# Adjacency tiles of 128 rows for the graph diffusion, and another table of how many diffusions stand in each block

## The reference

```python
R = S + jnp.eye(N); R = R / R.sum(-1, keepdims=True)
Z = 0; Xf = X; Xa = X
for n in range(2):
    probs = softmax((Xa @ W1.T @ W2.T) @ (Xa @ W3.T).T)
    A = probs * (in the top-p set of its row, p = 0.9);  A = A / A.sum(-1)
    Xf = R @ Xf                     # the diffusion, twice
    Xa = A @ Xa                     # the attention, twice
    Z = Z + Xf @ U1[n].T + Xa @ U2[n].T
```

## Time and profile before

| | |
|---|---|
| Time, median of 3 runs | 7123.94 us (7119.68 to 7130.17) |
| Profiled execution | 7131.35 us, its span 7129.6 us |
| Busy, share of the span | PE 64%, DVE 75%, ACT 30%, POOL 5% |
| Second attention pass | 1933 to 4957 us |
| TensorE clock granted, mean | 0.828 of full speed |
| L687, the diffusion's products | 834.5 us busy, 308.9 us idle before them, 301.1 of it until a DMA |

### The profile page before, as it was taken

One profiled execution on the slowest core, in us unless ns is written; L12 is line 12 of the kernel. 1 busy time (PEld: TensorE's weight loads), 2 busy tenths in 40 slices (PEclk: granted clock), 3 DMA queues, 4 the chain that ended last, 5 costly groups with the idle time before them and its releaser, 6 DMA issues. The chain is left out here.

```text
span 7129.6 us, 80171 instructions
## 1 busy us (share of the span) xinstructions
PE 4537.1 (64%) x27812; PEld 3255.7 (46%) x27812; DVE 5314.4 (75%) x13021; ACT 2161.8 (30%) x3033; POOL 344.0 (5%) x170
## 2 busy tenths in 40 slices
PE   5995688888665364523475588553337888835981
PEld 2442467676554354522464477453311222205981
DVE  4885577777448888887888899886349999974864
ACT  2332565656311011100132244222132222213541
POOL 0000000000110000000000000010000222020000
PEclk9997788888897787866787799786669999977995
DMA  5551000000032122111111122110103333303840
GB/s 171 202 199 57 1 2 1 1 1 1 21 132 97 57 86 85 75 40 43 58 66 57 50 87 93 59 58 17 29 16 130 107 110 109 110 26 144 292 161 29
DMA packets 192671, 549.28 MB, mean 77 GB/s; under 512 B 20027, under 2 KB 77126, under 8 KB 192126
## 3 DMA queue, kind: packets, MB, share of 16 engines
q1 hardware_dynamic: 187069, 539.58, 21.2%
q0 software_dynamic: 5120, 3.97, 0.2%
HBM read 526.73 MB, written 16.68 MB: 76 GB/s over the span
## 5 line engine op out<-in xcount | busy, mean ns | idle before, releaser
L655 PE MATMUL ps<-ident,arena 125*125 125x125 f32 x3200 | 562.9, 311 | 1161.4 <-DVEq L1139 1161.4
L655 PEld LDWEIGHTS ps<-ident,arena 125*125 125x125 f32 x3200 | 492.9, 224 | 1201.7 <-DVEq L1139 1201.7
L687 PE MATMUL ps<-arena 125*125 125x129 f32 x6400 | 834.5, 289 | 308.9 <-DMA arena<-in_adj_tiles 301.1
L663 PE MATMUL ps<-arena,turned 125*125 125x129 f32 x6400 | 943.7, 297 | 104.7 <-ACT turned L759 104.7
L1438 DVE SCALAR_TENSOR_TENSOR arena<-arena,pair 125x1000 f32<-125x1000 f32 x800 | 939.3, 1253 | 71.3 <-ACT arena L1401 71.3
L759 ACT ACTIVATE turned<-ps 125x500 f32<-125x500 f32 x800 | 464.4, 587 | 1699.4 <-PE ps L655 1698.2
L687 PEld LDWEIGHTS ps<-arena 125*125 125x125 f32 x6400 | 782.5, 199 | 380.6 <-DMA arena<-in_adj_tiles 298.1
L663 PEld LDWEIGHTS ps<-arena,turned 125*125 125x125 f32 x6400 | 869.3, 208 | 121.3 <-ACT turned L759 117.6
L1456 PE MATMUL ps<-arena 125*64 125x500 f32 x3200 | 765.0, 601 | 192.9 <-DVE arena L1438 192.8
L1092 DVE SCALAR_TENSOR_TENSOR arena<-arena,wt 125x5000 f32<-125x5000 f32 x80 | 434.1, 5427 | 194.6 <-issue 194.6
L1456 PEld LDWEIGHTS ps<-arena 125*64 125x64 f32 x3200 | 197.9, 137 | 756.9 <-DVE arena L1438 525.1
(11 more groups left out here) (343 smaller groups left out, 6073.1 us busy)
## 6 DMA issues: line engine op xcount, KB each, us to landing
arena<-in_adj_wide SPq DMA_DIRECT2D x400, 500.0 KB, 4.5
arena<-in_adj_tiles SPq DMA_DIRECT2D x400, 488.3 KB
arena<-in_adj_wide SPq DMA_DIRECT2D x100, 1000.0 KB, 4.8
x_saved<-arena SPq DMA_DIRECT2D x4, 2500.0 KB
arena<-x_saved SPq DMA_DIRECT2D x3, 2500.0 KB
arena<-att_saved SPq DMA_DIRECT2D x1, 2519.5 KB
arena<-in_x SPq DMA_DIRECT2D x1, 2500.0 KB
arena<-in_h SPq DMA_DIRECT2D x1, 2500.0 KB
```

The source lines that it names most:

```text
L655: mm = pe.transpose(banks_turn[:, g % 2, c * P:(c + 1) * P], work[b % DEPTH][:, j:j + P], ident[0:P, 0:P])
L663: mm = pe.matmul(acc_attend, turned[:, g % 2, c * P:(c + 1) * P], nodes(v_attend, FA)[:, j, :], start=(j == 0), stop=(j == NB - 1))
L687: mm = pe.matmul(acc_spread, ring[:, j * P:(j + 1) * P], values[:, j, :], start=(j == 0), stop=False)
```

## The change

Two things. The adjacency tiles of the diffusion are laid out in DRAM with 128 rows instead of 125, the last three zero, and each piece is loaded as 128 x 1000 into 128 rows of `ring`; the products still read 125 rows. And the table of diffusions per block is another; it still sums to 72 behind the first 8.

```diff
-SPREADS = (5, 3, [4] * 8 + [0, 3, 3] + [1, 1, 2, 1] * 6 + [2, 2, 0, 0, 0])
+SPREADS = (5, 3, [8, 8, 6, 6, 4, 0, 6, 6, 6, 6, 6] + [1, 0] * 10 + [0] * 9)
...
-                ring = rows(RING, N)
+                ring, padded_ring = rows(RING, N), rows(RING, N, 128)
...
-                            sp.dma_start(ring[:, q * 1000:(q + 1) * 1000],
-                                         adj_tiles[r * P:(r + 1) * P, q * 1000:(q + 1) * 1000])\
+                            sp.dma_start(padded_ring[:, q * 1000:(q + 1) * 1000],
+                                         adj_tiles[r * 128:(r + 1) * 128, q * 1000:(q + 1) * 1000])\
...
-    tiles = adj.reshape(NB, P, NB, P).transpose(0, 3, 2, 1).reshape(N, N)
+    tiles = _np.zeros((NB, 128, NB, P), _np.float32)
+    tiles[:, 0:P] = adj.reshape(NB, P, NB, P).transpose(0, 3, 2, 1)
+    tiles = tiles.reshape(NB * 128, N)
```

## The result

| | before | after |
|---|---|---|
| Time, median (4 runs each) | 7123.26 us (7119.68 to 7130.17) | 7066.28 us (7065.77 to 7071.5) |
| Ratio, 95% interval | | 0.992 (0.9903 to 0.9938) |
| Profiled execution, its span | 7131.35, 7129.6 us | 7065.77, 7064.0 us |
| L687, busy and idle before it | 834.5 and 308.9 us | 736.6 and 36.7 us |
| SP's first load of the pass to DVE's last signal of it | 3008.2 us | 2953.4 us |

What follows compares the result with a forecast made beforehand. It took DVE's chain of steps, and the start ahead of it, to bound the kernel. -33.5 (start) + 2.6 (cold logits) - 4.9 (step 15) = -35.8 us, from 7123.94 to 7088 us; range 7074 to 7105.

Steps and rivals of the forecast that it cites:

- `turn_query(0)`: Start of the pass: PE reaches its first query at 2007.3 and not 2040.8, -33.5 us.
- cold logits 0: First logits after PE idles: 5.28 us become 10.6 at half the clock; half of the 5.3 taken, +2.6 us.
- step 15: Late blocks: block 13's second diffusion delays DVE there; with at most one diffusion a block, -4.9 us.
- DVE's stalls: DVE's waits behind jumps: no term in the sum; only a rival made them longer, up to +72 us, chance 5%.
- What bounds the kernel: Second pass: DVE's chain from 2048 to 4957, the start before it; PE's 256.1 us of adjacency waits nearly all covered.
- A diffusion's time: 9.7 us each with a warm clock, at PE's own pace, needing 264 GB/s; load-bound ones had taken 18.8.
- What is late next is the scatter, at 2004: Start: diffusions end between 1988 and 2000, then POOL's query scatters gate; queries 3.3 us later, first query on PE at 2007.3.
- the bound of 2004: Start: POOL's scatter queue carries no packet from 2004 to 2022, so all scatters have landed by 2004.
- first rival: Start: scatters end sooner, having 16 engines and not five; gain up to 41.2 us, 7078 us in all, chance 18%.
- The sentence against it: Against scatters ending sooner: POOL issues one in about 1.5 us, and that does not change.
- The refined blocks: Blocks 0 to 10: 62 diffusions where they had 38 fit into PE's idle time within DVE's steps, cost zero.
- The rival of the program loads: Blocks 0 to 10: bursts on 16 engines delay DVE's code fetches ahead of L1092, +72 us, 7160, chance 5%.

Runs made afterwards that it cites:

- the repeat: The changed kernel run again, unchanged, beside later kernels: 7075.09 us against 7127.81 for the kernel before, ratio 0.9924.

## Why the prediction was wrong in size

| Term | forecast | measured |
|---|---|---|
| `turn_query(0)`, in the pass | 107.6 to 74.1: -33.5 | 107.6 to 67.2: -40.4 |
| cold logits 0 | +2.6 | 0 (+1.5 in the repeat, +2.3 where PE idled over 12 us) |
| step 15 | -4.9 | -5.1 |
| DVE's stalls | 0 (as a rival: longer) | -9.2 |
| sum in the pass | -35.8 | -54.8 |

**What bounds the kernel** was read rightly: DVE's chain from the first maxima on, and the start ahead of it. PE's 256 us of waiting for adjacency were nearly all covered, and went without a gain; the time came from the start, from step 15, and from something not forecast.

**A diffusion's time** was right: 9.7 us in the refined blocks. At the start it was right in some profiles, but for the first diffusion (11.9), and 11 to 14 in others; the load then moved 294 GB/s with the scatters in it, more than the 264 that were asked for.

**The start: the mis-sized term.** The step "What is late next is the scatter, at 2004" named the right gate and then took its time over from before, although that time had been measured beside a stream that is over by then in the changed kernel. The last scatter was issued 2.7 us sooner (61.7 in the pass, not 64.4) because its idle time of 5.39 us fell to 2.75; it landed in 3.3 us and not in 5.9, which is another 2.6; and the queries were there 2.1 us after SP asked for them, where the median of POOL's scatters had lent 3.3. (The last 0.5 us is the bound of 2004: the scatters had landed at 70.3 in the pass, not 70.8.) The forecast had this case as its first rival, bounded it by 41.2 us, and gave it 18%; it looked for the cause in 16 engines instead of five. The run with no diffusion ahead shows the scatter as quick with no adjacency at all, and both runs with six ahead show it landing late beside a stream on 16 engines, so it is the end of the stream that helps; for the 2.7 us ahead of the issue one of those two runs is an exception. The sentence against it, that POOL issues a scatter each 1.5 us and that does not change, was true of 39 scatters and false of the 40th, the one that counts.

**Cold logits.** The price was right (2.3 us in the rows alone, the kernels with none and with four ahead), but the full halving behind it was not: those logits took 7.62 us and not 10.6, and that half of 5.3 came true is luck. In the changed kernel's profile PE waits 0.97 us only, since its diffusions were slow, and pays nothing; in its repeat it waits 1.08 and pays 1.5.

**The refined blocks** cost nothing, as forecast: with 128 rows every attention from 0 to 10 begins 0.1 us after DVE's signal. The table alone showed how wide the margin is, attentions up to 90 us late without a stop of DVE.

**Step 15** gave 5.1 us. But the table alone, the rows alone and both give it alike (38.0 us in each for 43.1), so either half of the change would have done.

**The rival of the program loads had its sign reversed.** It looked at the right resource, DVE's waits behind jumps, and asked what a burst on 16 engines would add. The stall ahead of L1092 stayed as it was (134.0 to 135.3 us). What the forecast did not ask is what the stream of before was costing already: the stalls of 3.3 to 6.4 us in steps 9, 10, 17, 24 and 33 stood in the trace of before, and their instruction packets came 0.5 to 2.6 us later there than after. It also read the wrong rows: the packets in these stalls are of queue q14, not q8, and of the 9.9 us ahead of L1092 that it took for the price of a fetch (step 10), 6.9 stand there without a fetch in them once the hint is left out. The five stalls are 9.5 us shorter, small differences elsewhere take 0.3 back. That is 9.2 of the 19.0 us by which the forecast of the pass fell short; the start gives 6.9, the logits 2.6, and step 15 0.2, to 0.1 us of rounding.

**The range** was built from the start alone: its low end was the first rival less the spread of the runs. With the 9.2 us as a case of its own it would have held the time. That the repeat's 7075.09 us lies inside it is no merit of it, since the kernel before took 7127.81 beside it and not 7124.

## What to carry to other kernels

When a change shortens a stream of loads, every duration that was measured beside it may be too long for the changed kernel, also that of the thing that is late next; take the nearest row from a quiet stretch, and price the side effects of the old stream (small transfers, code fetches) as possible gains and not only as risks. A transfer whose number of rows has only a small divisor up to 16 keeps few engines busy for long, and what else uses those engines waits: padding 125 rows to 128 was worth it even where the faster load itself was hidden. Changing how much work fills a covered gap (the table) is worth running alone before it is kept: beside the rows it moved some 220 us of PE's work into the refined blocks (865 us of PE there with both parts, 642 with the rows alone) and no more than 4 us of time. And before a run is read, check that the edited line reaches the blocks it is about, or two runs of one program pass for two kernels.

## What the runs showed of the hardware

- POOL's scatters of 125 rows leave one in 1.49 us, with 0.30 idle between them. The 40th has 2.75 to 2.9 idle us ahead of it when adjacency is over, 3.84 when it is just ending (126 rows), and 5.4 beside adjacency at 30.6% or at 79.6% of the engines, but 2.95 in the second run of six ahead, at 56.6%. It landed in 2.9 to 3.4 us in the quiet (4.2 in two profiles) and in 5.2 to 6.0 beside the stream.
- A load of 125 x 65 numbers into an empty queue was there 2.1 us after its issue; behind pieces of adjacency the first of three had been 17.
- Each of DVE's five stalls compared has one 8 KB instruction packet in it, which starts 0.6 to 1.4 us into the stall in the changed kernel and 1.6 to 3.9 us into it in the kernel before; from there the stall lasts 1.6 to 2.5 us in both. That adjacency in the queues delays it is inferred from this.
- In blocks 9 to 11 a hint for the path not taken put three more instruction packets into the wait ahead of L1092 (9.7 us and not 6.8 in step 9) and cost 3 to 7 us a step. In the four later blocks that take the same path no run left it out.
- The same program ran its diffusions ahead at 9.7 us each on one chip and at 11 to 14 on another while POOL scattered. Whether that is the chip or the group of runs is open; its pass took 2941 us both times.
- The kernel with 128 rows and no hint in blocks 9 to 11 takes 7058 to 7059 us, with four or five diffusions ahead: 0.990 of the kernel before, and about 1 in 500 less than the changed one.
